# Queries' norm inside the exponential, rotary products summed by transposes, bias as a row of a product, PSUM banks by table

## The reference

```python
def _layer(x, wqkv, qs, ksc, wo, lg, lb, w1, b1, w2, b2):
    h = shift_token(x)
    q, k, v = jnp.split(h @ wqkv, 3, axis=-1)      # 8 heads of 64
    ...
    q = l2norm(q) * qs
    k = l2norm(k) * ksc
    q, k = rotary_xpos(q, k)                       # q * cos * scale + rotate_half(q) * sin * scale
    o = local_attention(q, k, v)                   # windows of 64: own window and the one before, masked softmax
    x = x + o @ wo
    h = shift_token(x)
    h = (h - mu) / jnp.sqrt(var + 1e-05) * lg + lb
    a, g = jnp.split(h @ w1 + b1, 2, axis=-1)      # 2 x 341 wide
    x = x + (a * jax.nn.gelu(g, approximate=False)) @ w2 + b2
    return x
```

## Time and profile before

| | |
|---|---|
| median of 3 runs | 1067.91 us |
| lowest, highest | 1066.7 us, 1068.65 us |
| profiled execution, first to last instruction | 1068.3 us |
| mean granted TensorE clock in it | 0.954 |
| moved by DMA | 25.63 MB, mean 24 GB/s |

### The profile page before, as it was taken

The page is one execution under the profiler, slowest core; times in us unless marked ns, Lnnn a source line. Parts: engine busy times, 40 slices in busy tenths (PEclk is TensorE's granted clock), DMA queues, the critical chain, the costliest instruction groups (busy, mean ns, idle before and its releaser), DMA issues. The chain is left out here.

```text
span 1068.3 us, 25986 instructions
## 1 busy us (share of the span) xinstructions
PE 929.2 (87%) x10152; PEld 560.7 (52%) x10152; DVE 872.8 (82%) x1244; ACT 786.6 (74%) x1897; POOL 695.8 (65%) x386
## 2 busy tenths in 40 slices
PE   5577698899889989999999989998989999987875
PEld 2223345446455565556564646465655666664463
DVE  6788987998889986999999988998898976754542
ACT  5448666886898859886999688877869877783740
POOL 3026615787588775898688859884866677763731
PEclk9788889899999989999999999999999999999986
DMA  7000100010000100000101100100000100110010
GB/s 229 11 6 10 26 1 6 17 33 9 16 16 22 38 20 25 22 24 4 35 12 26 27 13 14 31 21 17 17 22 20 27 6 17 26 27 1 21 31 11
DMA packets 22618, 25.63 MB, mean 24 GB/s; under 512 B 2869, under 2 KB 14815, under 8 KB 22495
## 3 DMA queue, kind: packets, MB, share of 16 engines
q1 hardware_dynamic: 22207, 23.81, 8.6%
q10 hardware_dynamic: 288, 0.14, 0.0%
HBM read 9.26 MB, written 2.10 MB: 11 GB/s over the span
## 5 line engine op out<-in xcount | busy, mean ns | idle before, releaser
L1062 DVE TENSOR_TENSOR_SCAN scan<-du,decay 128x1028 f32<-128x1028 f32 (+1 forms) x160 | 306.3, 1952 | 10.9 <-PE YY L1252 7.3
L768 POOL TENSOR_TENSOR rn<-ssc,expo 128x16 f32<-128x16 f32 x64 | 214.0, 3344 | 5.3
L764 POOL TENSOR_SCALAR ssc<-ss 128x16 f32<-128x16 f32 x64 | 62.4, 975 | 213.4 <-DVE ss L1119 212.8
L914 ACT ACTIVATE prob<-BB,nmax 128x128 f32<-128x128 f32 x472 | 165.7, 380 | 39.4 <-DVE nmax L1157 28.0
L859 ACT ACTIVATE decay<-delta,negA 128x1024 f32<-128x1024 f32 (+1 forms) x160 | 154.2, 986 | 18.4 <-DVE scan L1062 16.5
L773 POOL TENSOR_TENSOR qkc<-qkc,qks 128x1024 f32<-128x1024 f32 x64 | 159.6, 2493 | 2.8 <-DVE qks L1137 2.7
L1252 PE MATMUL YY<-scan,diag 64*64 64x512 f32 (+1 forms) x1280 | 143.1, 538 | 10.9 <-DVE scan L1062 10.9
L777 POOL TENSOR_TENSOR qkc<-qkc,rn 128x1024 f32<-128x1024 f32 x64 | 133.2, 2082 | 5.0
L1252 PE MATMUL AA<-wqkv,hT 128*128 128x512 f32 x256 | 128.8, 627 | 6.0 <-DVE qks L1137 3.1
L914 ACT ACTIVATION_READ_ACCUMULATOR prob<-BB,nmax 128x1 f32 x472 | 104.2, 221 | 0.0
L1119 DVE TENSOR_REDUCE ss<-sq 128x16 f32<-128x1024 f32 x64 | 77.1, 1205 | 29.6 <-ACT sq L877 29.6
(11 more groups left out here) (144 smaller groups left out, 1858.8 us busy)
## 6 DMA issues: line engine op xcount, KB each, us to landing
v_even<-v_odd SPq DMA_DIRECT2D x96, 128.0 KB, 2.3
x<-in_x SPq DMA_DIRECT2D x6, 256.0 KB, 3.4
wqkv<-in_wqkv SPq DMA_DIRECT2D x1, 1536.0 KB
xT<-in_xT SPq DMA_DIRECT2D x6, 256.0 KB, 3.0
out<-outb SPq DMA_DIRECT2D x6, 256.0 KB, 2.9
w<-in_w SPq DMA_DIRECT2D x1, 682.0 KB
xT<-in_xT SPq DMA_DIRECT2D x4, 128.0 KB, 2.6
x<-in_x SPq DMA_DIRECT2D x4, 128.0 KB, 3.5
```

The source lines that it names most:

```text
L768: pool.tensor_tensor(rn[:, q % 2, :], ssc[:, :], expo[:, 0:2 * HEADS], ALU.pow).then_inc(rn_sb, 1)
L914: ins = act.activation(prob[:, h, :], bank_of(q, a)[:, c * P:(c + 1) * P], ACT.Exp, bias=nmax[:, q % 2, h:h + 1], accum_out=den[:, q % 2, ...
L1062: dve.tensor_tensor_scan(state, step, a, 0.0, ALU.add, ALU.mult).then_inc(scan_sb, 1)
```

## The change

It changes six things.

1. Queries no longer get their norm from POOL. `rn` is handed to the exponential as its scale (one number per row and head), and DVE multiplies the negated maxima, now in `nraw`, by it, a small operation of 8 columns behind a wait for `raw_sb` (its own reduction) and `rn_sb`. The mask's value is -1e30 in place of -3e38. `rn` has four buffers in place of two.
2. The sum of cosine and sine products of the queries is made by PE: `qk_T` transposes both `qkc` and `qks` into the same place of PSUM, the second on top of the first. For the keys POOL adds and multiplies as before, on 512 columns in place of 1024.
3. `b2` becomes one more row of `w2`, against a row of ones in `hid` (a memset at the start). `residual` is left only for layer 1, where it adds the mamba output.
4. Which PSUM bank a step writes is read from tables: a pair out of `AA`, `BB`, `YY` for `qk_in`, `qk_T`, `scores`, `probs_T`, `up_gate`; `C` or `M` for the single ones.
5. All five order strings are new.
6. The setup steps `masks` and `tables` stand before mamba's first scan.

```diff
-MASKED = -3.0e38
+MASKED = -1.0e30
...
+PAIR_TABLES = {
+    "qk_in": "ABBAABABBBBBBBBBABBABABAAAAABABABBBBAABBBBBAAAAAAAAABBAYYAABYYYYBY",
...
+BANK_TABLES = {
+    "up_a": "MCMCCCCCMCCMCMCMCMCCMMMCCMMCCCCCCCMCMCMMCMCMCCMCMCMCCMCCMMCM",
...
 def banks_of(step, args):
-    banks = HOLDS.get(step, "")
-    return "Y" if banks == "B" and args[0] in LATE else banks
+
+    pairs, banks = PAIR_STEPS.get(step), BANK_STEPS.get(step)
+    n = nth(step, args)
+    return (pairs[0][n] if pairs else "") + (banks[0][n] if banks else "")
...
             def scale(q):
...
-                if q >= 2:
-                    pool.wait_ge(qk_sb, q - 1)
-                pool.tensor_tensor(rn[:, q % 2, :], ssc[:, :], expo[:, 0:2 * HEADS], ALU.pow).then_inc(rn_sb, 1)
+                if q >= RN_RING:
+                    pool.wait_ge(qk_sb, q - RN_RING + 1)
+                    pool.wait_ge(prob_sb, 2 * (q - RN_RING + 1))
+                pool.tensor_tensor(rn[:, q % RN_RING, :], ssc[:, :], expo[:, 0:2 * HEADS], ALU.pow).then_inc(rn_sb, 1)
 
             def rotate(q):
                 pool.wait_ge(rope_mul, 2 * q + 2)
-                both_qk = qkc[:, q % 2].rearrange("p a x -> p (a x)")
-                pool.tensor_tensor(both_qk, both_qk, qks[:, q % 2].rearrange("p a x -> p (a x)"), ALU.add).then_inc(rope_add, 1)
+                pool.tensor_tensor(qkc[:, q % 2, 1], qkc[:, q % 2, 1], qks[:, q % 2, 1], ALU.add).then_inc(rope_add, 1)
                 pool.wait_ge(rope_add, q + 1)
                 pool.wait_ge(rn_sb, q + 1)
-                all_heads = heads(both_qk)
-                pool.tensor_tensor(all_heads, all_heads, rn[:, q % 2, :].unsqueeze(2).to_broadcast((P, 2 * HEADS, DH)),
+                keys = heads(qkc[:, q % 2, 1])
+                pool.tensor_tensor(keys, keys, rn[:, q % RN_RING, HEADS:].unsqueeze(2).to_broadcast((P, HEADS, DH)),
                                    ALU.mult).then_inc(qk_sb, 1)
...
-                pool.tensor_tensor(rows, rows, row("b2", g, l), ALU.add).then_inc(xb2_sb, 1)
-                if l == 1:
-                    pool.wait_ge(xb2_sb, f + 1)
-                    pool.tensor_tensor(rows, rows, x1[:, g % X_RING, 0:tiles_of(g)], ALU.add).then_inc(xb1_sb, 1)
+                pool.tensor_tensor(rows, rows, x1[:, g % X_RING, 0:tiles_of(g)], ALU.add).then_inc(xb1_sb, 1)
...
-                        ins = act.activation(prob[:, h, :], bank_of(q, a)[:, c * P:(c + 1) * P], ACT.Exp,
-                                             bias=nmax[:, q % 2, h:h + 1],
+                        ins = act.activation(prob[:, h, :], bank_of("scores", q, a)[:, c * P:(c + 1) * P], ACT.Exp,
+                                             bias=nmax[:, q % 2, h:h + 1], scale=rn[:, q % RN_RING, h:h + 1],
                                              accum_out=den[:, q % 2, h:h + 1])
...
-                dve.tensor_reduce(nmax[:, q % 2, :].rearrange("p (c a) -> p a c", a=2),
-                                  pair(q)[:, :].rearrange("p (a c x) -> p a c x", a=2, x=P), AX.X, ALU.max,
-                                  negate=True).then_inc(max_sb, 1)
+                dve.tensor_reduce(nraw[:, q % 2, :].rearrange("p (c a) -> p a c", a=2),
+                                  pair("scores", q)[:, :].rearrange("p (a c x) -> p a c x", a=2, x=P), AX.X, ALU.max,
+                                  negate=True).then_inc(raw_sb, 1)
+                dve.wait_ge(raw_sb, q + 1)
+                dve.wait_ge(rn_sb, q + 1)
+                dve.tensor_tensor(nmax[:, q % 2, :], nraw[:, q % 2, :], rn[:, q % RN_RING, 0:HEADS], ALU.mult).then_inc(max_sb, 1)
...
-                for a in range(2):
-                    for c in range(PAIRS):
-                        for w in range(2):
-                            ins = pe.transpose(bank_of(q, w)[:, (a * PAIRS + c) * WIN:(a * PAIRS + c + 1) * WIN],
-                                               qkc[half(w), q % 2, a, c * P:(c + 1) * P], ident[half(w), half(w)])
...
+                for a, parts in ((0, (qkc, qks)), (1, (qkc,))):
+                    for n, part in enumerate(parts):
+                        for c in range(PAIRS):
+                            for w in range(2):
...
+                                ins = pe.matmul(bank_of("qk_T", q, w)[:, lo:lo + WIN], part[half(w), q % 2, a, c * P:(c + 1) * P],
+                                                ident[half(w), half(w)], start=a == 0 and n == 0 and c == 0, stop=last,
+                                                is_transpose=True, skip_group_check=True)
...
-                    mm((A[0], A[1], M)[c][0:n, 0:tok_of(g)], w1[:, l, HID + lo:HID + lo + n], bk(hnT, g)).then_inc(upg_ps, 1)
+                    mm(up_bank(f, c)[0:n, 0:tok_of(g)], w1[:, l, HID + lo:HID + lo + n], bk(hnT, g)).then_inc(upg_ps, 1)
```

672 lines of the change are left out of this document (340 added, 332 removed).

## The result

The changed kernel takes 1072.76 us (median of 5 runs, 1070.32 to 1075.85), the kernel before on the same chip 1067.49 (5 runs, 1066.7 to 1068.65). The ratio is 1.0056, 95% interval 1.0032 to 1.0080. The forecast of 1053 us said faster; it came out slower by 5.3 us.

The account below looks back on a forecast made before the run. The time was taken as PE's work plus 139.1 us in which PE has none. The terms +20 +4 +3 -3 -28 -11 = -15 against 1068.3 us gave 1053 us, with an 8-in-10 range of 1032 to 1088.

Parts of the forecast that it names:

- (b): ACT's 512 exponentials take their scale from memory: 51 us more ACT work, mostly hidden; +4 us, bounds 0 and +26.
- (a): PE transposes 24 pieces per tile in place of 16: 22.9 us of work; +20 us, bounds +8 and +46.
- (c): DVE gets 64 small products, each behind a wait: 14 us of work; +3 us, bounds 0 and +14.
- (d): POOL's add and product go to 512 columns, shortening the last tiles' path; -3 us, bounds -9 and +3.
- (e): PSUM banks chosen by table remove PE's waits for banks not yet emptied; -28 us, bounds 0 and -41.
- (f): At the head, the new order fills idle PE time with tiles 0 and 1; -11 us, bounds 0 and -25.
- R1: ACT takes over: the scale's price shows fully and PE's `probs_T` comes late; +21 us, 1089 us, chance 0.23.
- R2: PE's bank waits only change hands, the gain just paying for its transposes; 0, 1068 us, chance 0.13.
- R3: The tables remove all 41.0 us of PE's bank waits and the head brings 20; -42, 1026 us, chance 0.16.
- R4: More transposes lower PE's clock in the middle to 0.92, losing some 39 us; 1092 us, chance 0.04.

## Why the prediction was wrong, step by step

From the kernel before to the changed one the runs make a path, each step the difference of two medians: -10.4 (GpSimd's halves and the bias row), +11.5 (transposes), +12.4 (product), +25.6 (scale from memory), -33.8 (orders and banks): +5.3.

**(b) is the step that failed.** The size of the operand's work was nearly right: 51 us were forecast from the earlier trace rows, 45 measured. Wrong was "ACT still has 13% to spare, so most is hidden by PE's own queue: I take +4". It costs 25.6 us in the old orders, 32.5 in the new, and 26.7 alone on the kernel before. With +26, the upper bound that the step itself named, and all else as forecast, the sum is +7, 1075 us, within 3 us of the measured time. That the rest of the sum fits so well is partly luck: (a) was forecast 8.5 us too dear, (c) 9.4 too cheap, (d) gained 7.4 more than forecast and (e) with (f) 5 less, and these errors nearly cancel. The occupancy of ACT in the middle rose only to 534.10 of 650 us (82%), short of the 90% from which rival R1 was to decide; its price came in full without its condition. What the runs show in place of the cover is R1's path: `probs_T` comes late on PE. With the scale PE waits longer for `prob` by 17.0 us in the new order, 18.9 in the old and 12.9 on the kernel before, which is 64 to 78% of the idle time that the scale adds. ACT's 28 us of idle time ahead of the exponentials stood untouched when only this edit was made. A likely reason is that these waits come from the same round of work (scores, maximum, exponential, transposed probabilities, the bank of the next queries and keys) that the longer exponential delays, so that they move with it. The extra copy, outside this round, costs less than half as much for each us of ACT's busy time and leaves the waits for `prob` as they are. That the round is the whole cause isn't shown: without the maximum, an operand in the same place is worth 15.7 us for 43.8, as little as the copy.

Two signs that the prediction had named for being wrong both came: PE's idle time in the middle rose above 45 us, to 54.8, and ACT's waits for PE fell while PE's for `prob` rose.

By the rule of the Trainium skill, page "ScalarE: Activation LUTs", section "What ACT_TABLE_LOAD costs" (about 93 ns for each pointer operand), the traces agree nearly: 84 ns for each of two, and in exponentials of 128 columns too, which the row of before couldn't show. The prediction's estimate of 48 us from that page stands against 45 measured.

**(a)** +20 was forecast; it cost 11.5 in the old orders, with neither scale nor product beside it, and 4.3 in the new, with both. The work was 15.4 us in the new order and 16.3 in the old (62.0 and 45.7 for the transposes' line), and not 22.9: the forecast took the 44.8 ns of a piece from the whole run, in which the last piece counts with its full 230 ns. A run pays that once, and eight more pieces in it don't pay it again. Adding on top of what stands in PSUM didn't raise the price. PE's whole busy time grew still less, by 2.8 us (929.2 to 932.0) between the two kernels of the old orders, at a clock of 0.956 and 0.968 in the profiled executions. By these clocks 92.9 us of the span passed at the lower level with 16 pieces and 68.1 with 24. An estimate from that is that some 12 us of the added work came back by the clock. Why the clock rose isn't shown.

**(c)** +3 was forecast, 12.4 measured in the old orders, near the bound of 14. The products take 230 to 306 ns each where a reciprocal took 186, 306 in the kernel that this price is read from. They stand between maximum and exponential, and ACT's waits for the maximum grew with them by 8.6 us. With a constant scale (a) and (c) cost 23.9 us together in the old orders and 11.7 in the new; 23 was the forecast's sum.

**(d)** -3 was forecast, -9 its bound; -10.4 measured, together with the bias row, whose own cost was forecast at nothing. The 0.2 us of waits said nothing on how much the tile's path through GpSimd mattered. In the new order the short path is worth 56.2 us: with the long one PE waits 41.8 us for `qkc`, and 4.8 with the short one.

**(e) and (f)** -28 and -11 were forecast, -39 together; -33.8 measured for both. The runs part them only at the two ends. The last five blocks' banks alone are worth 26.8 us within the new order. The forecast named their mechanism (the waits for `gelus` and `hidden` in `M`) but not the clock that comes with it. The last `down` starts 1.3 us nearer to the end of the span, where 2 were to be seen. PE's idle time from 40 to 200 us fell to 36.2, where 30 was to be seen, at a clock of 0.88. Without the maximum, putting the head back recovered nothing, so the late first scan cost nothing there.

**The rivals.** R2's picture (waits change hands, 1068 us) and R1's price (slower by +26 for (b)) came out together. R3 needed PE to be idle for some 70 us; it was idle for 138.4. R4 fell: the clock hardly moved with more transposes. The medians of the runs with 16 and with 24 pieces are 0.957 and 0.963 in the old orders, 0.966 and 0.969 in the new, and 0.976 and 0.975 in the new with a constant scale (there the 24 come with the product too). These steps are as small as the spread of one kernel's runs. The Trainium skill, page "TensorE: Matmul & The Clock Gate", section "Part 4: PE-mode transpose", says that a transpose doesn't count as busy for the clock in the same way. The granted clock of these kernels, whose queues mix transposes with products, doesn't show it.

## What to carry to other kernels

Idle time on an in-order engine ahead of an instruction isn't cover by itself. Here 43 us of work behind 28 us of idle time cost 27, and the idle time stayed. Look whether its releaser depends on that same instruction one round earlier; in the round of a softmax that is likely, though it isn't shown here alone. So price a lengthened step by who waits for its result, and by the engine's share of busy time after that. And try the one edit alone on the old kernel before it is built into a new order.

The best version here that computes all of the reference doesn't make the maximum's product cheaper but drops the maximum: where inputs to a softmax are normalized and bounded, the reduction, its product and one of the exponential's two operands go together (1031.5 us, 3.4% under the kernel before). And an order that suits a short path can lose when the path grows: the new order with the old arithmetic is 17 us slower than the old order with it.
